# Graph-network kernel, first edge stage: a merged 128-row product over a 63-row window, whole-tile one-hots, every fifth batch placed by TensorE, one VectorE product to scale fetched rows

## What is computed

```python
dst = jnp.minimum((3125 * jax.random.uniform(..., (100000,)) ** 2.0).astype(jnp.int32), 99999)
_o = jnp.argsort(dst, stable=True)          # src and dst are put in this order
...
# layer 0
mi = jnp.concatenate([node_feats[src_bi], node_feats[tgt_bi], ef_bi], 1)    # both directions of each edge
h = jax.nn.relu(_layernorm(mi @ msg_w1 + msg_b1, ln1_g, ln1_b)) @ msg_w2 + msg_b2
agg = jax.ops.segment_sum(h, tgt_bi, num_segments=node_feats.shape[0])
# layer 1
p = jnp.exp(e - seg_max[src]);  p = p / segment_sum(p, src)[src]            # softmax over the edges of a source
agg = jax.ops.segment_sum(norm_h[src] * p[:, None], dst, num_segments=n)
```

## Time and profile before

| what | value |
|---|---|
| median of 3 runs | 5465.92 us (5465.03 to 5468.97) |
| profiled execution, its own time | 5450.14 us |
| its span, first to last instruction | 5448.2 us |
| instructions | 94725 |
| busy: PE, DVE, POOL, ACT | 86%, 84%, 75%, 67% |
| mean granted clock of TensorE | 0.911 |
| first edge stage, on POOL | about 86 to 2458 us |

### The profile page before, as it was taken

One profiled execution on the slowest core, in us unless ns is written; L12 is line 12 of the kernel. 1 busy time (PEld: TensorE's weight loads), 2 busy tenths in 40 slices (PEclk: granted clock), 3 DMA queues, 4 the chain that ended last, 5 costly groups with the idle time before them and its releaser, 6 DMA issues.

```text
span 5448.2 us, 94725 instructions
## 1 busy us (share of the span) xinstructions
PE 4679.2 (86%) x27130; PEld 3397.1 (62%) x27130; DVE 4596.6 (84%) x13376; ACT 3625.1 (67%) x12260; POOL 4070.7 (75%) x3716
## 2 busy tenths in 40 slices
PE   4899999999999999985888889588888886999995
PEld 3777777777777777765555555355555554455553
DVE  5999999999999999986888888688888877777776
ACT  4777777777777777762777777367777763555553
POOL 4788888888888888884777777577777764777776
PEclk7889999989899999997999989699999998999998
DMA  6867777777666666653777777467666762555553
GB/s 221 159 158 177 181 181 176 181 177 176 161 158 155 161 157 156 160 105 96 195 202 197 202 196 197 139 210 215 210 212 208 212 188 84 160 156 161 156 161 110
DMA packets 636916, 935.13 MB, mean 172 GB/s; under 512 B 105224, under 2 KB 346114, under 8 KB 635730
## 3 DMA queue, kind: packets, MB, share of 16 engines
q1 hardware_dynamic: 416690, 580.51, 34.4%
q0 software_dynamic: 219680, 348.31, 30.5%
HBM read 613.49 MB, written 314.95 MB: 170 GB/s over the span
## 4 chain that ended last, share of the span: by engine, by line
POOL 50%; issue 20%; PE 14%; DVE 8%; DMA 5%; ACT 2%; POOLq 0%; DVEq 0%; SPq 0%; ACTq 0%
POOL arena L1787 27%; POOL tab L1405 12%; POOL arena L1429 10%; DMA tab<-arena 3%; DMA arena<-T,srcI 2%; PE PS L2313 2%; PE PS L1974 2%; PE PS L2291 1%; PE PS L809 1%; PE PS L1018 1%; PE PS L1749 1%; PE PS L1020 1%; PE PS L1028 1%; PE PS L2303 1%; PE PS L1040 1%
## 5 line engine op out<-in xcount | busy, mean ns | idle before, releaser
L1787 POOL DMA_INDIRECT arena<-T,srcI x2112 | 2018.4, 956 | 797.8 <-issue 629.6
L1405 POOL DMA_INDIRECT tab<-arena x680 | 1117.4, 1643 | 230.7 <-issue 209.4
L1429 POOL DMA_INDIRECT arena<-T,srcI x784 | 800.6, 1021 | 270.7 <-issue 231.6
L1774 DVE TENSOR_TENSOR_SCAN arena<-arena,PS 128x512 f32<-128x512 bf16 x588 | 748.3, 1273 | 169.6 <-PE PS L2625 81.1
L1758 ACT ACTIVATE arena<-PS 128x512 f32<-128x512 f32 x588 | 347.9, 592 | 616.5 <-PE PS L1749 616.5
L1854 DVE TENSOR_SCALAR arena<-PS,nodeid 128x512 bf16<-128x512 f32 x908 | 627.1, 737 | 76.2 <-PE PS L1835 76.2
L2607 PE MATMUL PS<-arena 128*128 128x512 bf16 x2400 | 555.4, 382 | 0.0
L1974 PE MATMUL PS<-arena 128*128 128x396 bf16 x2800 | 540.0, 350 | 8.4 <-DVE arena L1854 7.2
L1018 PE MATMUL PS<-We,arena 65*128 65x256 f32 x1568 | 493.3, 397 | 62.2 <-DVE arena L1078 50.1
L809 PE MATMUL PS<-arena 128*128 128x448 bf16 x2184 | 535.1, 404 | 0.8 <-DVE arena L824 0.8
L1365 ACT ACTIVATE arena<-arena 128x128 bf16<-128x128 f32 x1568 | 459.5, 300 | 39.5 <-DVE arena L1078 39.5
(11 more groups left out here) (321 smaller groups left out, 10958.2 us busy)
## 6 DMA issues: line engine op xcount, KB each, us to landing
H<-arena SPq DMA_DIRECT2D x784, 256.0 KB, 2.4
arena<-keepR SPq DMA_DIRECT2D x294, 256.0 KB, 4.7
arena<-wF SPq DMA_DIRECT2D x98, 512.0 KB, 5.5
arena<-T,srcI POOLq DMA_INDIRECT x2896, 3.4
arena<-in_ea64T SPq DMA_DIRECT2D x98, 256.0 KB
arena<-sH SPq DMA_DIRECT2D x98, 256.0 KB
arena<-dH SPq DMA_DIRECT2D x98, 256.0 KB
arena<-S SPq DMA_DIRECT2D x98, 256.0 KB
```

Source lines behind the costliest of these rows:

```text
L1405: e.indirect_dma_start(out=tabs[k % KT], out_offset=at_rows(iA[b % 10][:, c:c + 1]), in_=X2[n % 3][:, c, :], in_offset=None, compute_op=AL ...
L1429: e.indirect_dma_start(out=Gs[b % NR][:, c, :], out_offset=None, in_=T0, in_offset=at_rows(srcI[:, CB * b + c:CB * b + c + 1])).then_inc(g ...
L1774: ins = e.tensor_tensor_scan(s[b % n][:, h, :], kR[g % 6][:, h0:h0 + CB * P], src[h], s[(b - 1) % n][:, h, CB * P - 1:CB * P] if b else in ...
L1787: e.indirect_dma_start(out=dst[:, c, :], out_offset=None, in_=T_tab, in_offset=at_rows(srcI[:, CB * b + c:CB * b + c + 1])).then_inc(gs.of ...
```

## The change

The window shrinks from 128 rows to 63, so that one product of 128 rows holds the 64 feature rows, the 63 window rows and one bias row. The stacked left side is the tile `eT`: its lower half is loaded as before, its upper half is the one-hot, written by DVE at partitions 64 to 127. The stacked right side is `Wt`, of which SP reloads 63 rows per group. Four matmuls per batch take the place of eight. The bound from which an edge is marked as outside follows: `out_w = rel >= WIN`. `pool_outside` itself is the same code in both kernels. `Spread(5, 36)` takes the place of `Spread(7, 26)`, its steps being spread over half steps. `dve_D` is one product over 1024 columns instead of five pieces, `act_Da` is gone, and `dve_A` makes `eq`, `OL` and `RH` in one instruction each.

```diff
+WIN = 63
 ...
-                e.tensor_scalar(out_w, rel, float(P), None, ALU.is_ge).then_inc(own.sem, own.up())
+                e.tensor_scalar(out_w, rel, float(WIN), None, ALU.is_ge).then_inc(own.sem, own.up())
 ...
-                e.tensor_scalar(wcol[:, :], d0B, small[:, 12, 0:1], -float(MID), ALU.add, ALU.add)
+                e.tensor_scalar(wcol[:, :], d0B, small[:, 12, 0:1], cols[:, 7:8], ALU.add, ALU.mult)
 ...
+                self.turns = [4 * M * k // 14 for k in range(14)]
 ...
-            pk = Spread(7, 26)
+            pk = Spread(5, 36)
 ...
-                e.dma_start(Tw[g % 2][:, 0:P], T0[bass.ds(v, P), P:2 * P]).then_inc(ld_t.of(g), 16)
-                e.dma_start(Tw[g % 2][:, P:2 * P], T0[bass.ds(v, P), 0:P]).then_inc(ld_t.of(g), 16)
+                e.dma_start(Wt[g % 2][64:64 + WIN, 0:P], T0[bass.ds(v, WIN), P:2 * P]).then_inc(ld_t.of(g), 16)
+                e.dma_start(Wt[g % 2][64:64 + WIN, P:2 * P], T0[bass.ds(v, WIN), 0:P]).then_inc(ld_t.of(g), 16)
 ...
                 for c in range(CB):
-                    e.matmul(psC[:, c * 2 * P:(c + 1) * 2 * P], eT[g % 2][0:65, h0 + c * P:h0 + (c + 1) * P],
-                             We[0:65, :], start=True, stop=False)
-                    ins = e.matmul(psC[:, c * 2 * P:(c + 1) * 2 * P], OT[b % 2][:, c * P:(c + 1) * P], Tw[g % 2],
-                                   start=False, stop=True)
+                    ins = e.matmul(psC[:, c * 2 * P:(c + 1) * 2 * P], eT[g % 2][:, h0 + c * P:h0 + (c + 1) * P], Wt[g % 2],
+                                   start=True, stop=True)
 ...
                 t = Gs[b % NR].rearrange("p c (h f) -> p (c h) f", h=2)
-                for k in range(C2 - ND):
-                    ins = e.tensor_scalar(t[:, k, :], t[:, k, :], rst[g % 3][:, o + k:o + k + 1], None, ALU.mult)
-                ins.then_inc(D.of(0), 1)
+                e.tensor_tensor(t, t, bf(rst[g % 3][:, o:o + C2], P), ALU.mult).then_inc(D.of(0), 1)
 ...
-                for c in range(C2):
-                    k = C2 * g + c
-                    e.tensor_scalar(OL[:, c, :], iotaf[:, :], loF[:, k:k + 1], None, ALU.is_equal)
+                e.tensor_tensor(eq, bc(iotaf[:, 0:NBLK], C2), bf(hiF[:, C2 * g:C2 * g + C2], NBLK), ALU.is_equal)
+                e.tensor_tensor(OL, bc(iotaf[:, :], C2), bf(loF[:, C2 * g:C2 * g + C2], P), ALU.is_equal)
 ...
-                for c in range(C2):
-                    k = C2 * g + c
-                    ins = e.scalar_tensor_tensor(out=RH[:, c, :, :], in0=bc(iotaf[:, 0:NBLK], 2), scalar=hiF[:, k:k + 1],
-                                                 in1=bf(first[:, c, :], NBLK), op0=ALU.is_equal, op1=ALU.mult)
+                ins = e.tensor_tensor(RH, eq.unsqueeze(2).to_broadcast([P, C2, 2, NBLK]),
+                                      first.unsqueeze(3).to_broadcast([P, C2, 2, NBLK]), ALU.mult)
 ...
+                if b >= 4:
+                    e.wait_ge(C.of(0), C.at(b - 4))
+                e.tensor_scalar(eT[g % 2][64:P, h0:h0 + CB * P], dR[g % 2][64:P, h0:h0 + CB * P], cols[64:P, 7:8],
+                                wcol[64:P, g:g + 1], ALU.mult, ALU.is_equal).then_inc(OTd.of(0), 1)
 ...
-                for k in range(C2 - ND, C2):
-                    ins = e.activation(t[:, k, :], t[:, k, :], ACT.Copy, scale=rst[g % 3][:, o + k:o + k + 1])
-                ins.then_inc(Da.of(0), 1)
```

More of the change, by code:

```diff
@@ L637, in dve @@
                 e.tensor_copy(d0I[:, :], d0B)
-                e.tensor_scalar(small[:, 12, 0:1], pcol[:, :], -float(NPAD), None, ALU.add).then_inc(own.sem, own.up())
+                e.tensor_scalar(small[:, 12, 0:1], pcol[:, :], -float(NPAD + 64 + MID), None, ALU.add)
+                e.tensor_scalar(cols[:, 7:8], pcol[:, :], float(NPAD + 64 + WIN), None, ALU.is_lt
+                                ).then_inc(own.sem, own.up())
                 e.wait_ge(own.sem, own.n)
-                e.tensor_scalar(wcol[:, :], d0B, small[:, 12, 0:1], -float(MID), ALU.add, ALU.add)
+                e.tensor_scalar(wcol[:, :], d0B, small[:, 12, 0:1], cols[:, 7:8], ALU.add, ALU.mult)
                 e.tensor_scalar(srcF[:, :], srcI[:, :], -float(MID), None, ALU.add)
@@ L741, in of_group, with at @@
                 return None
-            def at(self, i):
-                s, u = divmod(i - self.first, 2 * self.M)
-                return (s, u) if 0 <= s < self.n // 2 and u < 14 else (None, None)
+            def at(self, t):
+                s, u = divmod(t - 2 * self.first, 4 * self.M)
+                if not 0 <= s < self.n // 2 or u not in self.turns:
+                    return None, None
+                return s, self.turns.index(u)
             def act_cut_1(self, e, b, R2, O_):
@@ L839, in L0_edges @@
             kR = [arena.get(GE, dt=BF16) for _ in range(2)]
-            Tw = [arena.get(2 * P) for _ in range(2)]
-            OT = [arena.get(CB * P) for _ in range(2)]
+            Wt = [arena.get(2 * P) for _ in range(2)]
             r1, r2 = bank(2), [arena.get(CB, P) for _ in range(2)]
@@ L876, in L0_edges @@
             tab = take("tb", CB * len(pk.by_pool), KT, 16)
-            ok, C, t_, S1, V, S2, S3, sq, ex, OTd, D, Da = [take(n, NBAT) for n in (
-                "ok", "C", "t", "S1", "V", "S2", "S3", "sq", "ex", "OT", "D", "Da")]
+            ok, C, t_, S1, V, S2, S3, sq, ex, OTd, D = [take(n, NBAT) for n in (
+                "ok", "C", "t", "S1", "V", "S2", "S3", "sq", "ex", "OT", "D")]
             T, r_, scan, B, O_ = [take(n, NBAT) for n in ("T", "r", "scan", "B", "O")]
@@ L1064, in pe @@
                         pe_B(e, i - 7)
+                    pk.pe_step(e, 2 * i)
                     if 0 <= i - 2 < NBAT:
@@ L1259, in dve @@
                     e.memset(x2[:, :, P:XW], 0.0)
-                for t in eT:
-                    e.memset(t[64:65, :], 1.0)
+                for t in Wt:
+                    ins = e.tensor_copy(t, We[:, :])
+                ins.then_inc(s_wt, 1)
                 for i in range(NBAT + 11):
```

68 lines of the change are left out of this document (30 added, 38 removed).

## The result

The changed kernel takes 9444.6 us (median of 4 runs, 9439.5 to 9445.3) against 5466.0 us: a ratio of 1.7275, 95% interval 1.7245 to 1.7305. The forecast was 9340, range 8150 to 10400. Its profiled execution has a span of 9442.4 us, 3994 more than before.

What follows compares the result with a forecast made beforehand. POOL's unbroken list of indirect DMAs was taken to bound the first edge stage. 5450 + 4018 (guarded body) - 78 (scatters) - 50 (crowding) - 20 (waits) = 9320, by the runs' median 9336, said as 9340 us; range 8150 to 10400.

Steps and rivals of the forecast that it cites:

- The flag: First edge stage: window of 63 makes the count of marked edges nonzero (378), so the guarded body runs 196 times.
- The body's price: POOL, per run of `pool_outside`: 2.45 us wait, 15.0 for eight adds, 3.0 last landing; 20.5 us, times 196 = 4018.
- The last landing: End of the body on POOL: waiting for the last of eight adds to land, taken as 3.0 us.
- The landing: Body's DMA waits: skill estimates 2.15 us against 3.4 in the rows; using it makes the body some 1.2 us shorter.
- Spread, product, scaling, one-hots: First edge stage: ten fewer scattered batches save POOL 78 us; PE, ACT and DVE changes have nothing on the path.
- rival C: Guarded body isn't run, POOL stays the bound with 78 us less: 5388 us, faster by 1.4%; chance 0.04.
- the 390 named as a sign: PE, first edge stage: the merged product should stand at 4 per batch with about 390 ns each.
- Less crowding: POOL's scatters and gathers come near their minima with DVE and queues idle: at most 127 us, 50 taken.
- The sum: Whole kernel: profiled 5450 + 4018 - 78 - 50 - 20 = 9320, plus 16 for the runs' median; forecast 9340.
- A: Body on POOL: gather with an add costs as a plain gather; body 14.9 us, time 8240; chance 0.18.
- B: Body's adds go at their landings' pace, from one shared row or no overlap: 13900 us; mild form 10340; together 0.08.

Runs made afterwards that it cites:

- e1: Changed kernel with the outside bound set back from 63 to 128, so the guarded body isn't run, first chip: 5451.5 us, ratio 0.9983 to before.
- e2: Kernel before with only the outside bound changed from 128 to 63, window still 128 rows: 9452.0 us, 3989 over before.
- e3: Changed kernel with the body's eight indirect adds made plain gathers, without the add: 8515.3 us, 929 less.
- e7: Changed kernel with the bound back at 128 and both the old scaling and old one-hots, second chip: 6303.1 us, ratio 1.0279 to before.
- e9: Changed kernel with the bound back at 128, the same kernel as e1, run on the third chip: 6203.9 us, ratio 1.0120 to before.
- e4: Changed kernel with unmarked edges' index spread over 64 zero rows instead of all on row 3199: 9228.0 us, 217 less.
- e5: Changed kernel with the bound back at 128 and the old scaling (VectorE five pieces, ScalarE three), second chip: 6140.0 us, ratio 1.0022 to before.
- e12: Changed kernel with window loaded per 512-edge batch, padding unmarked, scaling split four pieces each between VectorE and ScalarE, third chip: 6133.2 us, ratio 0.9981 to before.
- e8: Changed kernel with the bound back at 128 and every seventh batch on TensorE instead of every fifth, second chip: 6208.7 us, ratio 1.0125.

## Why the prediction was right, point by point

**The flag.** Right: the narrow window makes a count nonzero, and one flag runs the body for all 196 batches. e1 and e2 show it from both sides: set back in the changed kernel it takes 3993 us away, set in the old one it adds 3989.

**The body's price.** 20.5 us forecast. From the changed kernel's rows: issuing 2476.2 / 196 = 12.6, its idle time 793.3 / 196 = 4.0, waits after it (699.0 + 14) / 196 = 3.6, the two index instructions 97.2 / 196 = 0.5: together 20.8, less 0.3 for a gap that stood there anyway, 20.5. The parts held: 1579 ns for an add (1577 taken), 2.45 us on average from the last gather's end to the first add (2.45 taken; half of them are under 2.1). The last landing was taken too short, 3.0 for 3.7 us; that was made up by two gaps of 0.30 us too many in the sum (eight between eight adds, and the one that stood there anyway), so that the last tenths agree by luck. The reason given for 1577, one packet per row because of the add, is borne out by e3 as far as the packets go (144 against 32 for a transfer); that they are what costs POOL the time wasn't tried apart. `ok` of a batch comes eight POOL steps before its scatter, not four, which changes nothing.

**The landing.** The estimate from the Trainium skill, "DMA: Bandwidth & Descriptors", section "Anatomy of one DMA — SWDGE (gpsimd) path", 2.15 us, is for a transfer of this size; here the profile gives 4.4 us from issue to landing for the adds. The measurement decides. The prediction also understated the difference: it set 2.15 against waits that begin when POOL's instruction ends. Counted from its start, as the 3.4 and 4.4 are, it would have made the two waits 1.2 and 0.6 us, and the body 3.7 us shorter, not 1.2.

**Spread, product, scaling, one-hots.** "Nothing on the path" was right while the body covers them, since POOL alone set the stage. As a statement on the change without the body it was not: rival C's 5388 was a price for that case, and e1 gave 5451. The merged product's records (1560, eight per batch where the code has four matmuls) took 525 ns each and not the 390 named as a sign, at the granted clock of 0.64; in e1, at 0.89, they took 385.

**Less crowding: the term that failed.** It was to give 50 us, in that DMA instructions near their minima when VectorE idles two thirds of the time. They got longer: gathers 1021 to 1062 ns, scatters 1643 to 1673, 50 us to the bad. Where they start explains why idle time didn't help. `ok` is raised at the end of the body, so VectorE's work on a batch falls just on the scatters and gathers that follow (1.85, 2.41, 1.37 us in the timeline above): VectorE is busy for 35% of the stage, but 564 of the 768 gathers and 527 of the 640 scatters began while it worked. Of the adds, in a quiet stretch, 1344 of 1568 began with VectorE idle, and these took 1545 ns on average; 69 began under a tensor_tensor of 1 us or more with both inputs in SBUF, and took 2168. All adds together have a median of 1538 ns over a minimum of 1530:

```profile
L1412 POOL DMA_INDIRECT arena<-T,arena x1568: 1530/1538/2567, 87.5 to 6368.9; - x196
...
DMA to landing us min/median/max: 4.0/4.4/9.4
```

And VectorE's new whole-tile instructions hold POOL longer than the old small ones: e2, with the old ones, kept 1021 and 1637. The prediction had named the rule for it, of the Trainium skill, "SBUF — State Buffer", section "Who interferes with whom": a tensor_tensor with both inputs in SBUF contends with GpSimd's reads. It then let the rule change nothing. The runs agree with it: in the table under e1 a DMA instruction takes 1.2 to 1.4 times as long under a tensor_tensor of that kind, and not longer under the one that reads PSUM, and with both forms old (e7) a gather is 75 ns and a scatter 51 ns shorter than in e9. In the changed kernel the difference from e2 is 784 x 0.040 + 640 x 0.036 + 1568 x 0.019 = 84 us, all parts of the change taken together.

**The sum.** Forecast for the profiled execution + 3870, measured + 3994. The 124 us too little are the crowding (100), some 17 us of longer gaps and waits on POOL, and 7 us in the later stages.

**The rivals.** A is dead by L1412's 1579 ns, and e3 shows that the add makes them. B in its strong form is dead too: the adds follow each other at 1.84 us and land 4.4 us after their start, so they overlap. (The argument against it misread a row: in the earlier trace rows the scatters start 3.2 us apart and not 1.88, with a gather between; with a landing of 5.15 us they overlap even so.) Its first half was not empty, though: e4 shows that 128 reads of one row do cost, 1.07 us a body, in the landing and not in the pace. C's trigger is right, its price 63 us too low: "POOL stays the bound" didn't hold, as e1's chain shows.

**Open.** Why the same kernel stands at 0.9983 of before on the first chip and at 1.0120 on the third. POOL's instructions take the same time on both (1084 and 1075 ns, 1674 and 1669), but its waits for ScalarE's copies are 39.1 us in e1 and 144.7 in e9. Most of what the third chip takes longer lies elsewhere: up to the end of the first edge stage 2458 us in e1 and 2567 in e9, after it, in code that no experiment touches, 2991 and 3627, with waits there that the profile puts down to another core or an unknown queue and that e1 doesn't have. For the kernel before there is no trace from the second or third chip, so where it loses its 670 us isn't known. What e5 to e12 show of the parts of the change is therefore shown for those two chips alone.

## What to carry to other kernels

Before pricing what a change does to an inner loop, put the inputs through every bound that it moves: here a window of 63 against a largest distance of 118, and of 64 in a real group, turned on a fallback for everything. It cost 3993 us, where the rest was to gain 78 and gained 11. A fallback behind one flag for all the work is a cliff; padding should never be able to trip it. And where engines run close to each other, a saving on one can turn into a wait for another: e7's short DMA instructions gained nothing, and e8's 40 scatters more cost nothing. Look at the chain of work after a change, too: by its busy time and fixed gaps alone POOL still seemed to be the bound of e1.

## What the runs showed of the hardware

- An indirect gather with an add costs POOL 1.58 us where the same gather without it costs 0.98 (128 rows of 512 bytes, changed kernel and e3); it leaves 144 packets in the queue instead of 32.
- POOL waits 1.07 us longer for the last add when all its 128 rows are read from one and the same row than when they are spread over 64 (changed kernel and e4); this was not expected.
- A POOL DMA instruction that starts under a 1.22 us VectorE tensor_tensor with two SBUF inputs takes longer: gathers 1386 ns on average against 984 with VectorE idle, scatters 1954 against 1574; under an equally long one that reads PSUM, 977 and 1578 (e1). One was seen at 2.06 us.
- TensorE, busy in 41% of the stage, was granted 0.64 of its full clock there and 0.93 after it: between its two levels of 1.2 and 2.4 GHz, nearer the lower. Its 128x256 matmuls took 525 ns there and 385 in e1.
